# Splitting an attention output projection around the first block of running maxima, and reordering VectorE's work beside it

## The chip, the core and the metric

The kernel runs on one core of one Trainium2 chip. A core has four computing engines with instruction streams of their own: TensorE (PE, matrix products, written to PSUM banks), VectorE (DVE), ScalarE (ACT) and GpSimd (POOL). A fifth stream, SyncE (SP), issues most DMA transfers. The engines meet only at semaphores. The metric is the device time of one execution in microseconds; the median of several runs counts.

## The reference

Sixteen sequences of 512 tokens with 256 features go through one attention layer and one mixture-of-experts layer.

```
x = layernorm(x + attention(x))        # 16 heads of 16; each token sees 39 earlier offsets: 0..32, 48, 64, 96, 128, 192, 256, 384
    scores = q . shift(k, offset) / 4 + pos_bias ; alpha = softmax(scores)
    out    = (sum alpha * shift(v, offset)) * sigmoid(x @ Wgate + bgate) @ Wout + bout
x = layernorm(x + experts(x))          # router: relu(x @ rw1) @ rw2, top 2 of 8, capacity 1024; two-layer experts
```

Products are made from half-precision pairs: a value is split in a high and a low half, and three products (high by high, high by low, low by high) are added up.

## The kernel before

Three stages follow one another: `attention` with the router and the scatter of the tokens (to about 1300 us), `experts`, and `combine`, the last normalization. The change is in `attention` alone.

Attention works on one sequence, a batch, at a time, in a software pipeline written out by hand. An iteration has 16 slots. The table `SLOTS_OF` says which parts stand in a slot, and `AHEAD` of which batch: while the projections (`proj`) and the maxima (`maxp`) are those of the next batch, the scores and values are those of this one, and the gate, the output projection (`outp`) and the router (`rout`, `rank`) those of the last or the one before. Each engine walks through the same slots. TensorE does a part in its own slot, the others one slot later, or by as many as `LATER` says. Within a slot an engine first does what its `head` function finds in the tables, then the parts in their listed order, and then, on ScalarE, its `tail`. A slot is no barrier: it only fixes the order in which each engine issues its work, and the semaphores do the rest. An engine that waits holds up all that is behind it in this order.

These parts stand around the change:

- **Output projection.** Part `t` transposes the gated attention output and ScalarE copies it to `featT` (L860). Part `w` (L754 on TensorE) multiplies by `wout`: 24 products, two PSUM banks of 12. VectorE adds the residual (L1036), takes statistics of the four row tiles (`bn_stats` L1041, `bn_aggr` L1044), GpSimd makes the inverse deviation (L1147 to L1152), and ScalarE normalizes (part `y`, L909) and casts (L914). Then comes the router, from the same rows.
- **Near maxima, `near0` to `near3`, far maxima, `far0` and `far1`.** TensorE computes scores of the next batch (L720 for the bias, L730 the products; L740 and L748 for far), two banks each, and VectorE takes the maximum of each group (L1022, L1026).
- **Six pairs of score and value blocks, k = 0 to 5** (two far, four near), placed by the tables `SCORES_AT` to `EVAC_AT`. For a pair TensorE makes the scores (`scores`), ScalarE the exponentials (`weights`, L831 and L832, `EXP_AT`), VectorE and GpSimd the low halves, one half of the heads each (`split_weights`, L415, `SPLIT_AT`), and TensorE multiplies by the values (`values`, L666, `VALUES_AT`). A far result is copied by ScalarE (`evacuate_far`, L823), a near one is added by VectorE to what came back of the far results (`merge`, L958 and L963); both follow `EVAC_AT`.
- **The way of the far results.** SyncE's head at slot 6 waits for both far copies, stores `o_far` to memory in four transfers (L465), waits until they have landed, and loads them in another order as `o_back` (L468). The first near merge waits for this load. SyncE issues ahead of it the row loads of the next batch's queries and keys (L500).

All projections, maxima and transposes share three PSUM banks `gp` in rotation. Each use takes the bank of the third use before it, once that has been drained by its reader (`unit` on TensorE, `gp_drained`). `near` parts acquire both their banks before their first product:

```
units = [unit(n, "maxp", part, e) for e in range(2)]
```

A near value block can only begin when the merge of the one before it is done, since there is one pair of banks `o`:

```
alone.wait_ge(plo_dve, n.at(UNIT_PAIRS, k + 1))
alone.wait_ge(plo_pool, n.at(UNIT_PAIRS, k + 1))
...
    alone.wait_ge(merged, n.at(TILES, k - FAR_PAIRS))
```

The orders that result in this stretch are, before the change:

- TensorE: output projection, near0, values 2, scores 3, near1, near2, near3, far0, values 3, scores 4, far1, router transposes.
- VectorE: split 2, rank, two residual adds, statistics, near0, first near merge, near1, split 3, near2, near3, `y` low half, far0, rank, second merge, far1.
- ScalarE: gate and value casts, `featT` copies, exponentials 2, copy of far result 1, `y`, exponentials 3.

Of the kernel before, what the change touches and what calls it, by code (L numbers as in the profile page):

```python
# [57 lines left out]
SLOTS_OF = {  # L58
    0: [("proj", "qk0"), ("gate", "den1"), ("gate", "inv1")], 1: [("proj", "qk1"), ("gate", "mul")], 2: [("proj", "vg0")],
# [12 lines left out]
         ("dve", "rout", "h0"): 2, ("dve", "rout", "h1"): 2, ("dve", "rout", "h2"): 2, ("dve", "rout", "h3"): 2}  # L72

UNITS = {("feat", "x"): 2, ("proj", "qk0"): 2, ("proj", "qk1"): 2, ("proj", "vg0"): 2, ("proj", "vg1"): 2,
         ("outp", "t"): 2, ("outp", "w"): 2, ("maxp", "near0"): 2, ("maxp", "near1"): 2, ("maxp", "near2"): 2,
         ("maxp", "near3"): 2, ("maxp", "far0"): 2, ("maxp", "far1"): 2,
         ("maxp", "t"): 1,
         ("rout", "t"): 2, ("rout", "h0"): 2, ("rout", "h1"): 2, ("rout", "h2"): 2, ("rout", "h3"): 2,
         ("rank", "l"): 1, ("rank", "c"): 1}

SCORES_AT = [-1, 0, 5, 7, 10, 12]
EXP_AT = [[-1, 1, 5, 8, 11, 13], [0, 1, 5, 8, 11, 13]]
SPLIT_AT = [1, 2, 6, 9, 12, 14]
VALUES_AT = [2, 4, 7, 10, 13, 16]
EVAC_AT = [3, 5, 8, 11, 14, 16]

GATED = {"den0": (0, 2), "inv0": (0, 2), "den1": (2, 4), "inv1": (2, 4)}
GATE_STEPS = len(GATED)
# [43 lines left out]
def wait(eng, sem, value):  # L132

    if not isinstance(value, int) or value > 0:
        eng.wait_ge(sem, value)
# [122 lines left out]
def attention(nc, g):  # L258
    ctx = ExitStack()
    with ctx:  # L260
# [160 lines left out]
        def _(sync):  # L421
# [18 lines left out]
            def head(n, h):  # L440
                if (n.c, h) == (B, 2):
                    first_expert()
                if not n.in_range():
                    return
                if h == 0 and n.shift(2).in_range() and not (n.i is None and n.c + 2 >= B):
                    load_x(n.shift(2))
                if h == 1:

                    wait(sp, pv_done, n.at(UNIT_PAIRS))
                    sp.wait_ge(v_stored, n.at(16, 16))  # L450
                    if n.i is None and n.c == 0:
                        sp.wait_ge(pad_in, 32)
                    for u in range(2):
                        half = PAIRS * VW
                        src = bass.AP(v_dram[n.par].tensor, half * u, [[2 * half, 2 * BLOCK], [2 * half * BLOCK, N // BLOCK], [1, half]])
                        dst = v_near[2 * BLOCK * u:2 * BLOCK * (u + 1), :, u, :, :]
                        sync.dma_start(dst.rearrange("w b h c -> w b (h c)"), src).then_inc(v_near_in, 16)
                if h == 6:

                    wait(sp, o_in, n.at(16))  # L460
                    sp.wait_ge(far_out, n.at(FAR_PAIRS, FAR_PAIRS))
                    for r4 in range(4):
                        dst = o_dram.rearrange("(a g r) c -> r a g c", g=4, r=4)[r4]
                        src = o_far[BLOCK * r4:BLOCK * (r4 + 1), :, :, :].rearrange("a g h c -> a g (h c)")
                        sync.dma_start(dst, src).then_inc(o_stored, 16)  # L465
                    wait(sp, merged, n.at(TILES))
                    sp.wait_ge(o_stored, n.at(64, 64))
                    sync.dma_start(o_back[:, :, :, :].rearrange("p t h c -> p t (h c)"), o_dram.rearrange("(t p) c -> p t c", p=P)).then_inc(o_in, 16)  # L468
                if h == 9:

                    if n.i is not None or n.c > 0:
                        drained(sp, n.shift(-1), "outp", "w", 1)
                    sync.dma_start(xres[:, :, :], g["x_rows"][bass.ds(n.at(N), N), :].rearrange("(t p) d -> p t d", p=P)).then_inc(xres_loaded, 16)

            def proj(n, part):
# [88 lines left out]
        def _(pe):  # L564
# [189 lines left out]
            def outp(n, part):  # L754
                if part == "t":
                    pe.wait_ge(og_hi, n.at(1, 1))
                    transposes(n, "outp", "t", 0, lambda t, c: og16[:, 0, t, P * c:P * (c + 1)])
                    pe.wait_ge(og_lo, n.at(1, 1))
                    transposes(n, "outp", "t", 1, lambda t, c: og16[:, 1, t, P * c:P * (c + 1)])
                elif part == "w":  # L760
                    drained(pe, n, "outp", "t", 0)
                    drained(pe, n, "outp", "t", 1)
                    for u in range(2):
                        bank, is_full = unit(n, "outp", "w", u)
                        for t in (2 * u, 2 * u + 1):
                            last = terms(lambda a, c: featT[:, a, c, P * t:P * (t + 1)], lambda b, c: wout[:, b, c, :],
                                         bank[:, D * (t % 2):D * (t % 2 + 1)])
                        last.then_inc(is_full, 1)
# [45 lines left out]
        def _(act):  # L814
# [101 lines left out]
            def rout(n, part):  # L916
                if part == "t":

                    transposed(n, "rout", lambda: full(act, n, "outp", "w", 1))
                else:  # L920
                    for k in range(2):
                        ht = 2 * int(part[1]) + k
                        bank = full(act, n, "rout", part, k)
                        wait(act, hid_lo, n.at(HT, ht - 3))
                        if ht == 0:

                            act.wait_ge(qk_split, n.at(4, 12) if n.i is not None else min(n.at(4, 12), 4 * B))
                        if ht == 0 and n.i is None and n.c == 0:
                            act.wait_ge(biases_in, 80)
                        if ht == 0 and (n.i is not None or n.c > 0):  # L930
                            full(act, n.shift(-1), "rank", "l", 0)
                        nc.scalar.activation(hid16[:, 0, ht, :], bank[:, :], ACT.Relu, bias=br1[:, ht:ht + 1], scale=1.0 / WS)  # L932
                        gp_done(nc.scalar.activation(rows32[:, ht % 4, :], bank[:, :], ACT.Relu, bias=br1[:, ht:ht + 1], scale=1.0 / WS),  # L933
                                n, "rout", part, k)
# [10 lines left out]
        def _(dve):  # L945
# [81 lines left out]
                                                        AX.X, ALU.max, negate=True), n, "maxp", part, e)  # L1027

            def outp(n, part):
                if part == "w":  # L1030
                    wait(dve, y_stored, n.at(16))
                    wait(dve, yh_ready, n.at(1))
                    for u in range(2):
                        bank = full(dve, n, "outp", "w", u)
                        dve.wait_ge(xres_ready, n.at(1, 1))
                        gp_done(nc.vector.scalar_tensor_tensor(y32[:, 2 * u:2 * u + 2, :], bank[:, :].rearrange("q (t d) -> q t d", t=2), 1.0 / WS,  # L1036
                                                               xres[:, 2 * u:2 * u + 2, :], ALU.mult, ALU.add), n, "outp", "w", u)
                    for u in range(2):
                        drained(dve, n, "outp", "w", u)
                    for t in range(TILES):  # L1040
                        nc.vector.bn_stats(stats[:, t, :], y32[:, t, :]).then_inc(ln_step, 1)  # L1041
                    alone.wait_ge(ln_step, n.at(TILES, TILES))
                    for t in range(TILES):
                        nc.vector.bn_aggr(mv[:, t, :], stats[:, t, :]).then_inc(var_ready, 1)  # L1044
                elif part == "y":
                    dve.wait_ge(yh_ready, n.at(1, 1))
                    nc.vector.tensor_tensor(y16[n.par][:, :, D:2 * D], y32[:, :, :], y16[n.par][:, :, 0:D], ALU.subtract).then_inc(yl_ready, 1)
# [76 lines left out]
        def _(gpsimd):  # L1124
# [13 lines left out]
            def outp(n, part):  # L1138
                if part == "t":

                    pool.wait_ge(xres_loaded, n.at(16, 16))
                    if n.i is None and n.c == 0:
                        pool.wait_ge(biases_in, 80)
                    nc.gpsimd.tensor_tensor(xres[:, :, :], xres[:, :, :], g_bo, ALU.add).then_inc(xres_ready, 1)
                elif part == "w":
                    pool.wait_ge(var_ready, n.at(TILES, TILES))
                    nc.gpsimd.tensor_scalar(veps[:, :], mv[:, :, 1], LN_EPS, 0.0, ALU.add, ALU.max)  # L1147
                    nc.gpsimd.tensor_scalar(nmr[:, :], mv[:, :, 0], -1.0, 0.0, ALU.mult, ALU.add).then_inc(veps_ready, 1)
                    pool.wait_ge(veps_ready, n.at(1, 1))
                    nc.gpsimd.tensor_tensor(rstd[:, :], veps[:, :], halfneg[:, :], ALU.pow).then_inc(rstd_ready, 1)  # L1150
                    pool.wait_ge(rstd_ready, n.at(1, 1))
                    nc.gpsimd.tensor_tensor(nmr[:, :], nmr[:, :], rstd[:, :], ALU.mult).then_inc(nmr_ready, 1)  # L1152
# [557 lines left out]
```

## Time and profile before

| what | value |
|---|---|
| median of 3 runs | 1766.84 us (1765.27 to 1768.31) |
| the profiled execution | 1772.04 us, of which the span from first to last instruction is 1770.3 us |
| TensorE busy, of the span | 1355.1 us (77%) |
| VectorE, ScalarE, GpSimd busy | 968.0, 902.0, 711.6 us |
| mean granted TensorE clock | 0.793 of full speed |

A row of the timeline gives the start in us from the span's start, the duration, engine, line, operation, output and input, and how many instructions are merged in it. In brackets stands how long the engine sat idle before it, and what ended that idle time. "issue" means that the engine waited for nothing that the profile shows. PE stands for matrix products and PEld for weight loads. A window row gives the stretch, its length, the busy time of each engine with its instructions, the granted clock (1.00 is 2.4 GHz, 0.50 is 1.2 GHz), and the DMA share and rate.

### The profile page before, as it was taken

Reading aid. Unit: us, or ns where it says so; the run is one execution under the profiler, and the core shown is the slowest. Engines: PE = TensorE matmul, PEld = TensorE weight load, DVE = VectorE, ACT = ScalarE, POOL = GpSimd, SP = SyncE. Lnnn points to the kernel's source line nnn. Section 1 sums busy time; section 2 is a strip of 40 time slices with the busy share of each in tenths; the row PEclk is TensorE's granted clock in tenths of the full one; section 3 lists DMA queues with packets and bytes.
Section 4 is the critical chain, followed back from the end, with each engine's and each line's share of the span. In section 5 each row is a group of like instructions: output and inputs, shape, how many; then the busy total and the mean of one; then the engine's idle time right before and its main releaser. Section 6 shows DMA issues by size and latency. Waiting matters only on the chain. (4 is left out here: it accounts for less than half of the span.)

```text
span 1770.3 us, 69102 instructions
## 1 busy us (share of the span) xinstructions
PE 1355.1 (77%) x31232; PEld 867.7 (49%) x31232; DVE 968.0 (55%) x2079; ACT 902.0 (51%) x1551; POOL 711.6 (40%) x653
## 2 busy tenths in 40 slices
PE   3556687786978888787787969787753999999960
PEld 1334354444545454555455545454432666666640
DVE  3225456564656755566565746656553555555426
ACT  4134364453746546464544636454543655555517
POOL 5123144353636445364443626344332133333346
PEclk9567696777868778787777869676766999999985
DMA  7655263533426353453634425252322344444239
GB/s 198 167 143 126 84 150 86 128 95 106 118 76 162 89 126 90 100 126 89 151 71 112 96 83 140 67 137 54 103 37 86 84 96 96 96 96 96 37 36 380
DMA packets 194694, 195.49 MB, mean 110 GB/s; under 512 B 61711, under 2 KB 178527, under 8 KB 191152
## 3 DMA queue, kind: packets, MB, share of 16 engines
q1 hardware_dynamic: 176208, 167.44, 35.9%
q0 software_dynamic: 15360, 15.10, 5.5%
q10 hardware_dynamic: 2832, 8.52, 1.2%
q8 instruction: 246, 4.03, 1.0%
q14 instruction: 48, 0.39, 0.1%
HBM read 115.63 MB, written 86.25 MB: 114 GB/s over the span
## 5 line engine op out<-in xcount | busy, mean ns | idle before, releaser
L415 POOL TENSOR_TENSOR p<-p 128x512 f16<-128x512 f32 x96 | 130.2, 1356 | 262.7 <-ACT p L832 262.6
L860 ACT COPY featT<-gp 128x1024 f16<-128x1024 f16 x96 | 93.0, 1023 | 270.3 <-PE gp L577 270.3
L1169 POOL DMA_INDIRECT disp<-y,sidx x128 | 187.8, 1467 | 55.7 <-issue 37.8
L1441 POOL DMA_INDIRECT xln<-y,place x64 | 103.4, 1615 | 222.3 <-DVE y L1581 203.7
L584 PE MATMUL gp<-featT,wr 128*128 128x512 f16 x768 | 186.0, 398 | 5.2 <-issue 2.9
L415 DVE TENSOR_TENSOR p<-p 128x512 f16<-128x512 f32 x96 | 83.0, 865 | 194.0 <-ACT p L832 193.9
L831 ACT ACTIVATE p<-st 128x512 f16<-128x512 f32 x192 | 116.8, 609 | 79.1 <-PE st L629 45.5
L1538 ACT ACTIVATE h<-up,v_near 128x512 f16<-128x512 f32 x128 | 88.2, 689 | 130.8 <-issue 124.0
L1156 POOL TENSOR_TENSOR x<-xin,x 128x1024 f16<-128x1024 f32 x16 | 34.0, 2127 | 276.1 <-ACT x L867 276.1
L1591 DVE TENSOR_TENSOR h<-h 128x512 f16<-128x512 f32 x128 | 88.7, 694 | 72.8 <-ACT h L1539 72.8
L629 PE MATMUL st<-qs,ks 49*64 49x32 f16 (+1 forms) x4096 | 102.2, 197 | 33.0 <-issue 32.9
L584 PEld LDWEIGHTS gp<-featT,wr 128*128 128x128 f16 x768 | 73.1, 101 | 100.8 <-issue 24.0
L584 PE MATMUL gp<-featT,wqk 128*128 128x512 f16 x384 | 115.9, 473 | 6.6 <-issue 5.5
L832 ACT ACTIVATE p<-st 128x512 f32<-128x512 f32 x192 | 118.0, 615 | 0.0
L932 ACT ACTIVATE hid<-gp,br 128x512 f16<-128x512 f32 x128 | 90.6, 708 | 53.3 <-DVE hid L1054 27.8
L1054 DVE TENSOR_TENSOR hid<-rows,hid 128x512 f16<-128x512 f32 x128 | 103.9, 855 | 14.2 <-ACT rows L933 14.2
L1005 DVE RECIPROCAL og<-og 128x512 f32<-128x512 f32 x32 | 107.3, 3353 | 1.1
L1131 POOL TENSOR_TENSOR qk<-rows,qk 128x512 f16<-128x512 f32 x64 | 73.5, 1157 | 82.3 <-ACT rows L884 81.8
L958 DVE TENSOR_TENSOR ob<-o,o_back 128x136 f32<-128x136 f32 x128 | 31.9, 291 | 133.1 <-DMA o_back<-o_dram 96.6
L1022 DVE TENSOR_REDUCE m_near<-gp 128x8 f16<-128x512 f32 x128 | 81.8, 680 | 30.7 <-PE gp L730 30.5
L629 PEld LDWEIGHTS st<-qs,ks 49*64 49x64 f16 (+1 forms) x4096 | 67.9, 120 | 58.9 <-issue 36.5
L1026 DVE TENSOR_REDUCE m_far<-gp 128x16 f16<-128x512 f32 x64 | 41.2, 686 | 94.4 <-PE gp L748 94.4
(191 smaller groups left out, 3046.1 us busy)
## 6 DMA issues: line engine op xcount, KB each, us to landing
v_near<-v_dram SPq DMA_DIRECT2D x32, 528.0 KB, 7.8
qk_dram<-qk SPq DMA_DIRECT2D x64, 256.0 KB, 3.6
o_dram<-o_far SPq DMA_DIRECT2D x64, 136.0 KB
o_back<-o_dram SPq DMA_DIRECT2D x16, 544.0 KB, 4.2
v_dram<-vs SPq DMA_DIRECT2D x16, 528.0 KB, 3.2
v_far<-v_dram SPq DMA_DIRECT2D x64, 132.0 KB
disp<-y ACTq DMA_DIRECT2D x8, 1040.0 KB, 7.1
rows<-disp SPq DMA_DIRECT2D x16, 520.0 KB, 3.6
```

Of the source, the lines that this page charges most:

```text
L415: engine.tensor_tensor(p16[:, b, 1, :], p32[:, b, :], p16[:, b, 0, :], ALU.subtract).then_inc(is_split, 1)
L584: last = nc.tensor.matmul(dst, lhs(a, c), rhs(b, c), start=(k == 0), stop=(k == len(todo) - 1))
L629: last = nc.tensor.matmul(banks[e][64 * u + first:64 * (u + 1), P * z + BLOCK * b:P * z + BLOCK * (b + 1)], key[rows[e], p, lo - BLOCK + f ...
L831: nc.scalar.activation(p16[:, b, 0, :], bank[:, :], ACT.Exp)
L832: nc.scalar.activation(p32[:, b, :], bank[:, :], ACT.Exp).then_inc(exp_ready, 1)
L860: gp_done(nc.scalar.copy(featT[:, i, :, :].rearrange("f c t -> f (c t)"), bank[:, :].bitcast(F16)), n, stage, PART_OF_T[stage], i)
L932: nc.scalar.activation(hid16[:, 0, ht, :], bank[:, :], ACT.Relu, bias=br1[:, ht:ht + 1], scale=1.0 / WS)
L1005: nc.vector.reciprocal(v, v).then_inc(og_step, 1)
L1054: nc.vector.tensor_tensor(hid16[:, 1, ht, :], rows32[:, ht % 4, :], hid16[:, 0, ht, :], ALU.subtract).then_inc(hid_lo, 1)
L1169: nc.gpsimd.indirect_dma_start(out=disp[:, :], out_offset=bass.IndirectOffsetOnAxis(ap=sidx[:, t, k:k + 1], axis=0), in_=y16[n.par][:, t, ...
L1441: nc.gpsimd.indirect_dma_start(out=xln[:, :], out_offset=bass.IndirectOffsetOnAxis(ap=place[:, gr, t:t + 1], axis=0), in_=y[:, gr, t, :], ...
L1591: nc.vector.tensor_tensor(h16[:, gr, 1, h, :], h32[:, h % 2, :], h16[:, gr, 0, h, :], ALU.subtract).then_inc(h_lo, 1)
```

## The change

The output projection becomes two parts, `w0` and `w1`, one bank each, with near0 between them. The residual add goes with each, and the statistics become a part of their own, `s`, behind both, for VectorE and GpSimd. VectorE's order becomes: residual add 0, near0, residual add 1, statistics, near1, first near merge, near2, near3, split 3, `y` low half, far0. On TensorE scores 3 move behind near1, and values 3 ahead of far0. On ScalarE the copy of far result 1 moves ahead of the second half of the value casts, the `featT` copies and exponentials 2. SyncE's reload of `xres` waits for `w1` in place of the second bank of `w`. The bank rotation changes with the order: near0 now takes banks between those of w0 and w1.

```
-    6: [("outp", "w"), ("maxp", "near0")],
+    6: [("outp", "w0"), ("maxp", "near0"), ("outp", "w1"), ("outp", "s")],
...
-         ("outp", "t"): 2, ("outp", "w"): 2, ("maxp", "near0"): 2, ...
+         ("outp", "t"): 2, ("outp", "w0"): 1, ("outp", "w1"): 1, ("maxp", "near0"): 2, ...
...
-SCORES_AT = [-1, 0, 5, 7, 10, 12]
+SCORES_AT = [-1, 0, 5, 8, 10, 12]
-SPLIT_AT = [1, 2, 6, 9, 12, 14]
-VALUES_AT = [2, 4, 7, 10, 13, 16]
-EVAC_AT = [3, 5, 8, 11, 14, 16]
+SPLIT_AT = [1, 2, 6, 10, 12, 14]
+VALUES_AT = [2, 4, 7, 9, 13, 16]
+EVAC_AT = [3, 4, 9, 11, 14, 16]
...
-                        drained(sp, n.shift(-1), "outp", "w", 1)
+                        drained(sp, n.shift(-1), "outp", "w1", 0)
...
-                elif part == "w":
-                    drained(pe, n, "outp", "t", 0)
-                    drained(pe, n, "outp", "t", 1)
-                    for u in range(2):
-                        bank, is_full = unit(n, "outp", "w", u)
+                elif part[0] == "w":
+                    if part == "w0":
+                        drained(pe, n, "outp", "t", 0)
+                        drained(pe, n, "outp", "t", 1)
+                    for u in (int(part[1]),):
+                        bank, is_full = unit(n, "outp", part, 0)
...
             def outp(n, part):
-                if part == "w":
-                    wait(dve, y_stored, n.at(16))
-                    wait(dve, yh_ready, n.at(1))
-                    for u in range(2):
-                        bank = full(dve, n, "outp", "w", u)
-                        dve.wait_ge(xres_ready, n.at(1, 1))
-                        gp_done(nc.vector.scalar_tensor_tensor(..., n, "outp", "w", u)
-                    for u in range(2):
-                        drained(dve, n, "outp", "w", u)
+                if part[0] == "w":
+                    if part == "w0":
+                        wait(dve, y_stored, n.at(16))
+                        wait(dve, yh_ready, n.at(1))
+                        dve.wait_ge(xres_ready, n.at(1, 1))
+                    u = int(part[1])
+                    bank = full(dve, n, "outp", part, 0)
+                    gp_done(nc.vector.scalar_tensor_tensor(..., n, "outp", part, 0)
+                elif part == "s":
+                    for u in range(2):
+                        drained(dve, n, "outp", f"w{u}", 0)
                     for t in range(TILES):
                         nc.vector.bn_stats(stats[:, t, :], y32[:, t, :]).then_inc(ln_step, 1)
```

On GpSimd the part `w` is renamed to `s`. No instruction is added or taken away on any engine.

## Rows read from the trace of the kernel before

**Rows 1.** Busy time of TensorE on the page: us, share, instructions.

```profile
PE 1355.1 (77%) x31232; PEld 867.7 (49%) x31232; DVE 968.0 (55%) x2079; ACT 902.0 (51%) x1551; POOL 711.6 (40%) x653
```

**Rows 2.** Waits over the span: waiting line, releaser, us, times, longest.

```profile
DVE ob L958 <- DMA o_back<-o_dram: 96.6, 16, 12.8
...
PE gp L720 <- DVE m_near L1022: 77.7, 33, 9.6
...
PE gp L740 <- DVE m_near L1022: 14.2, 16, 0.9
```

**Rows 3.** Timeline of TensorE in batch A, projection at 944.11.

```profile
944.11 2.78 PE L584 MATMUL gp<-wout,featT 128*128 128x256 f16 x24
946.88 0.39 PE L720 MATMUL gp<-near_bias,sel_rest 32*128 32x512 f16 x2
...
948.09 0.73 PE L666 MATMUL o<-v_near,p 128*32 128x66 f16 x64
...
952.41 0.39 PE L720 MATMUL gp<-near_bias,sel 32*128 32x512 f16 x2
...
958.64 0.61 PE L720 MATMUL gp<-near_bias,sel 32*128 32x512 f16 x2 [5.20 <-DVE m_near L1022]
...
962.96 0.39 PE L740 MATMUL gp<-far_bias,sel 32*128 32x256 f16 x2 [0.88 <-DVE m_near L1022]
...
967.06 0.82 PE L666 MATMUL o<-v_near,p 128*32 128x34 f16 x57 [1.67 <-issue]
967.81 0.29 PE L624 MATMUL st<-sel,near_bias 64*128 64x128 f16 x2
```

**Rows 4.** Timeline of VectorE in batch A.

```profile
946.92 0.69 DVE L1036 SCALAR_TENSOR_TENSOR y<-gp,xres 128x512 f32<-128x512 f32 x1 [0.19 <-PE gp L584]
...
949.16 0.38 DVE L1044 BATCH_NORM_AGGREGATE mv<-stats 128x2 f32<-128x6 f32 x4
...
956.86 0.51 DVE L958 TENSOR_TENSOR ob<-o,o_back 128x136 f32<-128x136 f32 x2 [6.15 <-DMA o_back<-o_dram]
```

**Rows 5.** Timeline of ScalarE in batch A.

```profile
940.67 0.42 ACT L892 CAST vs<-vg 128x256 f16<-128x256 f32 x1 [3.54 <-DVE vg L982]
...
941.91 1.90 ACT L860 COPY featT<-gp 128x1024 f16<-128x1024 f16 x2
...
945.84 0.71 ACT L823 COPY o_far<-o 128x272 f32<-128x272 f32 x2
...
951.58 2.07 ACT L909 ACTIVATE y<-y,nmr,rstd 128x256 f32<-128x256 f32 x4 [4.93 <-POOL nmr L1152]
...
956.13 0.61 ACT L832 ACTIVATE p<-st 128x512 f32<-128x512 f32 x1
```

**Rows 6.** Timeline of SyncE's DMA issues in batch A.

```profile
944.30 0.89 SPq L500 DMA_DIRECT2D ks<-qk_dram  x2
946.62 2.54 SPq L465 DMA_DIRECT2D o_dram<-o_far  x4
952.29 0.38 SPq L468 DMA_DIRECT2D o_back<-o_dram  x1
```

**Rows 7.** Timeline of GpSimd in batch A: its half of split 3.

```profile
956.82 1.16 POOL L415 TENSOR_TENSOR p<-p 128x512 f16<-128x512 f32 x1 [5.28 <-ACT p L832]
```

**Rows 8.** Timeline of TensorE in batch B, projection at 717.34.

```profile
717.34 4.45 PE L584 MATMUL gp<-wout,featT 128*128 128x256 f16 x24
...
730.12 0.61 PE L720 MATMUL gp<-near_bias,sel 32*128 32x512 f16 x2 [2.74 <-DVE m_near L1022]
```

**Rows 9.** Timeline of ScalarE in batch B: the last of exponentials 3.

```profile
731.03 0.61 ACT L832 ACTIVATE p<-st 128x512 f32<-128x512 f32 x1
```

**Rows 10.** Timeline of VectorE in batch B: the first near merge.

```profile
728.35 0.50 DVE L958 TENSOR_TENSOR ob<-o,o_back 128x136 f32<-128x136 f32 x2 [2.74 <-DMA o_back<-o_dram]
```

**Rows 11.** Windows in batch A: PE, PEld, DVE, ACT, POOL busy, clock, DMA share, GB/s.

```profile
952.00:954.00 2.00, 1.44 (x96) 0.95 (x84) 0.00 (x0) 1.91 (x5) 0.00 (x0) 0.78 0.26 49
958.00:979.00 21.00, 14.23 (x558) 9.94 (x559) 10.50 (x29) 2.80 (x4) 0.00 (x0) 0.50 0.04 11
```

More of the change, by code:

```diff
@@ L74 @@
 UNITS = {("feat", "x"): 2, ("proj", "qk0"): 2, ("proj", "qk1"): 2, ("proj", "vg0"): 2, ("proj", "vg1"): 2,
-         ("outp", "t"): 2, ("outp", "w"): 2, ("maxp", "near0"): 2, ("maxp", "near1"): 2, ("maxp", "near2"): 2,
+         ("outp", "t"): 2, ("outp", "w0"): 1, ("outp", "w1"): 1, ("maxp", "near0"): 2, ("maxp", "near1"): 2, ("maxp", "near2"): 2,
          ("maxp", "near3"): 2, ("maxp", "far0"): 2, ("maxp", "far1"): 2,
@@ L917, in rout @@
                 if part == "t":
-                    transposed(n, "rout", lambda: full(act, n, "outp", "w", 1))
+                    transposed(n, "rout", lambda: full(act, n, "outp", "w1", 0))
                 else:
@@ L1029, in outp @@
             def outp(n, part):
-                if part == "w":
-                    wait(dve, y_stored, n.at(16))
-                    wait(dve, yh_ready, n.at(1))
-                    for u in range(2):
-                        bank = full(dve, n, "outp", "w", u)
-                        dve.wait_ge(xres_ready, n.at(1, 1))
-                        gp_done(nc.vector.scalar_tensor_tensor(y32[:, 2 * u:2 * u + 2, :], bank[:, :].rearrange("q (t d) -> q t d", t=2), 1.0 / WS,
-                                                               xres[:, 2 * u:2 * u + 2, :], ALU.mult, ALU.add), n, "outp", "w", u)
-                    for u in range(2):
-                        drained(dve, n, "outp", "w", u)
+                if part[0] == "w":
[5 more added lines that the diff above has]
+                    bank = full(dve, n, "outp", part, 0)
+                    gp_done(nc.vector.scalar_tensor_tensor(y32[:, 2 * u:2 * u + 2, :], bank[:, :].rearrange("q (t d) -> q t d", t=2), 1.0 / WS,
+                                                           xres[:, 2 * u:2 * u + 2, :], ALU.mult, ALU.add), n, "outp", part, 0)
+                elif part == "s":
+                    for u in range(2):
+                        drained(dve, n, "outp", f"w{u}", 0)
                     for t in range(TILES):
@@ L1144, in outp @@
                     nc.gpsimd.tensor_tensor(xres[:, :, :], xres[:, :, :], g_bo, ALU.add).then_inc(xres_ready, 1)
-                elif part == "w":
+                elif part == "s":
                     pool.wait_ge(var_ready, n.at(TILES, TILES))
```

## The prediction

> **What bounds the kernel.** I read four views: the page's busy times, the list of waits, the timelines of two batches engine by engine, and windows for the clock. The chain that ended last is no help, since it covers only the last stage, which the change leaves alone. TensorE is busy for 1355.1 us [rows 1], and in every steady iteration of attention it is the engine with the least idle time, so a microsecond of its idle time is worth about one of the total, if the wait is not put back elsewhere. The list of waits shows where its idle time is: before near1 to near3 it stood 77.7 us, and before far0 14.2 us, until VectorE's near maxima had drained a bank [rows 2]. That is 91.9 us over the 15 iterations that make near maxima for a next batch, 6.1 us each. VectorE isn't slow there, it is stuck. Its first near merge stood 96.6 us, 16 times, for the reload of the far results [rows 2], and near1's maxima are queued behind this merge.
>
> Two batches show the range. In batch A TensorE ends near1 at 953.4 and stands 5.20 us before near2, 0.88 before near3 and 0.88 before far0, 6.96 in all [rows 3]. (The 0.88 before near3 is not among the rows; it is the same wait on the near reduction as before far0.) VectorE had waited 6.15 us for the load and merged at 956.86 [rows 4]. In batch B the first of these waits is 2.74 us [rows 8], so 4.50 in all, with the merge at 728.35 [rows 10].
>
> **What is moved, and what is late next.** The change adds no instruction. Its whole effect is which wait ends last. I follow batch A.
>
> *ScalarE's copy of far result 1* costs 0.71 us [rows 5], and it is moved ahead of the second value casts, the `featT` copies and exponentials 2. ScalarE was idle for 3.54 us before 940.67 [rows 5], but values 1 end only about 0.3 us before that, so only some 0.2 us of the copy is covered. I charge about 0.5 us to the `featT` copies, which end at 943.81 and release the projection at 944.11 [rows 3, 5]: TensorE starts it 0.3 us late. Exponentials 2 and split 2 are as late.
>
> *The way of the far results* gets earlier. The copy ended at 946.55 and SyncE stored at 946.62 [rows 5, 6]. Now the copy ends near 941.2, and SyncE is held by its own row loads until 945.19 [rows 6]. So the stores can start 1.4 us earlier and no more. They meet these loads in the DMA engines, so the gain at landing lies between 0 and 1.4 us, and I take 0.7. The load itself took 4.57 us from issue to merge [rows 4, 6]. The store of `y` and the reload of `xres`, which were issued during it, come later now, so I take another 0.4 off, with 0 and 0.7 as ends. The data is there at 955.8 in place of 956.86.
>
> *The projection halves.* 24 products took 2.78 us, near0 1.21 [rows 3]. The sum stays. w0 ends at 945.85, near0 at 947.05, and w1, which needs the bank that residual add 0 drains at about 947.2, ends at 948.65. VectorE does near0's maxima in 1.25 us from 947.2, residual add 1 to 949.45, and the statistics to 951.3, against 949.54 before [rows 4]: 1.8 us later. All of the chain to GpSimd, `y` and exponentials 3 is late by this 1.8. They ended at 956.74 [rows 5] and now end at 958.5. GpSimd's half of split 3 takes 1.16 us [rows 7] and ends at 959.7.
>
> *TensorE.* Values 2 and near1 run without a wait to 950.3, scores 3 with their 1.9 us of "issue" to 953.9, and near2 finds its banks drained: the 5.20 us are gone. near2 ends at 955.0. VectorE did near1's maxima by 952.6 and merges at 955.8 for 1.0 us. It reads near2's first bank by 957.5, and only then can near3 start: a wait of 2.5 us. near3 ends at 958.8, its maxima at 960.1, and VectorE's half of split 3, now queued behind them, at 960.8. Values 3, which stood behind far0 and so had far0 as cover, now start there: a wait of 2.0 us. From here 1.0 us of values and 2.16 us of far0 (962.96 to 965.12) bring scores 4 to 964.1, without any issue stall. Before it was 967.81, less the 1.67 of "issue" [rows 3], 966.1. Batch A gains 2.0 us: 6.96 of waits go, and 0.3, 2.5 and 2.0 come.
>
> *Batch B* was less late at the merge, while its exponentials 3 ended at 731.64 [rows 9]. Its projection ran at half clock, 4.45 us [rows 8]. Here the statistics are 1.3 us later, exponentials 3 end at 732.95, GpSimd's split at 734.1, and 3.2 us behind it scores 4 start at 737.3. Before, far0 started 4.3 us behind near2, as in A, at 734.4, and scores 4 without issue stalls at 737.6. It gains 0.3 us, as the chain through `y` decides it.
>
> *The sum.* The mean wait of 6.1 us per batch lies between B's 4.5 and A's 6.96, at 0.65 of the way, so the mean gain is 0.3 + 0.65 x 1.7 = 1.4 us, in 15 iterations 21 us. While TensorE stands at a semaphore, its instruction stream can catch up. Stalls named "issue" (1.90 in the middle of scores 3, 1.67 in values 3 of batch A) lie in the blocks of tiny products, and now values 2, near1, scores 3 and near2 follow one another without a pause. I charge 0.3 us a batch, 4 us, between 0 and 1 us a batch. No other wait takes over later in the iteration: the far maxima, the router transposes, the transposed maxima and the row loads behind them keep their order and all shift together. The profiled execution would go from 1772.04 to 1755, by 0.96%. On the median 1766.84 this is 1750.
>
> **The clock.** TensorE's granted clock was already at a mean of 0.78 of full speed in 952 to 954, while near1 still ran, and stayed at 0.50, 1.2 GHz, from 958 to 979 [rows 11]. In this stretch the engine was busy for 14.23 us, with tiny products in the main. So the fall began before the 5.20 us stand, and I count on no help from its going. The Trainium skill (TensorE: Matmul & The Clock Gate, Part 1) says that idle time brings the clock down to 1.2 GHz and sustained activity back up. By it, cutting the long stand in two would keep 2.4 GHz, and the sum would be near 1711; by the rows it stays at 1750.
>
> **Rivals.**
>
> 1. *The clock stays up.* The longest stand falls from 5.2 to some 2.5 us. near1 at 2.4 GHz took 1.03 us, near2 at 1.2 GHz 1.28 by the same timeline: a fifth. Of the 14.23 us in the low stretch some 2.8 would go, in 14 batches 39 us, so 1711, and with part of it 1711 to 1733. For it: the stand is the longest idle time of the iteration. Against: the clock at 952 to 954, and that it doesn't rise in the busy part of the 21 us.
>
> 2. *The output projection no longer lifts the clock (slower).* Batch B's projection began at 1.2 GHz and took 4.45 us, and the clock rose within or behind it. Cut in two by near0, it may leave the clock down until the router's hidden layer. Then w1 costs 0.8 more, near0, values 2 and near1 0.7, and scores 3 0.5, about 2 us a batch, and the statistics are later by most of it, which puts values 3 off by another 1. Three times 14 is 42 us against a gain of 17: 1792 at the worst, and 1771 where only the half of the batches that are like B suffer. It decides from 1.2 us a batch on.
>
> 3. *A wait for a wait (no change).* Values 3 without far0 as cover may wait as long as near2 did. In B it nearly does. If the far results land no earlier and exponentials 3 are late by 1 us more than I count, A gains 0.5 us and B loses 0.7: 1764 to 1769.
>
> **How the numbers follow.** Forecast, a gain of 0.3 to 1.9%: 0.62. Rival 1: 0.10. Rival 2: 0.14. Rival 3: 0.14. The bounds of the sum are 0.4 to 2.2 us a batch, 1734 to 1761. The range reaches to rival 3, to 1768, and on the low side to 1733, and leaves rivals 1 and 2 outside for the most part. A change of 0.2% (3.5 us) is about what a measurement of this kernel can tell from none. Faster: the forecast, rival 1 and a little of rival 3, 0.73. Same: most of rival 3 and the edge, 0.12. Slower: 0.15.
>
> **What the profile after would show.** Right: no wait of the near1 and near2 bias products (L720) on the near maxima above 1 us, one before near3 of 1 to 3 us, none before far0; a wait of 2 to 4 us of values 3 (L666) on a split (L415); the first merge's wait for the load down from 6 to about 3 us; ScalarE's `y` 1 to 2 us later after the start of the projection; scores 4 starting near 20 us after the start of the projection in batches like both A and B, where it was 22.0 in A without the issue stall. Wrong: if values 3 wait over 5 us, if the low clock starts with the projection in most batches, or if new "issue" time eats the gain.

## The result, and the profile after

The changed kernel takes 1759.91 us in the median of 20 runs, the kernel before 1767.68 in 20 runs beside them. The ratio is 0.9949, with a 95% interval from 0.9931 to 0.9966: 0.5% faster. Forecast were 1750 us and 0.96%, with a range from 1733 to 1768. The time is inside the range and the sign is right; the gain, 7.8 us by the medians, is about half of what was forecast, and its interval excludes 0.96%. The two executions that were profiled took 1772.04 and 1759.34 us, 12.7 us apart, since the one of the kernel before ran 4 us longer than its median.

The list of waits of the changed kernel. Its lines L720 and L740 are still the near and far bias products, L666 the values, L1023 the near maxima and L959 the first instruction of a merge:

```profile
DVE ob L959 <- DMA o_back<-o_dram: 44.8, 14, 6.9
...
PE gp L720 <- DVE m_near L1023: 31.1, 18, 5.4
...
PE o L666 <- DVE p L415: 28.7, 14, 2.5
...
PE o L666 <- POOL p L415: 14.3, 3, 9.7
```

The stand before the near products fell from 77.7 us in 33 waits to 31.1 in 18, and that before far0 (14.2) is gone but for one of 0.9 [rows 2]. In its place values 3 wait for a split. Of the 14.3 us for GpSimd's half, 9.7 us are one wait in the last iteration, where near maxima no longer exist; the kernel before had 9.0 us there.

Now one batch like A, with the projection at 325.91. TensorE:

```profile
325.91 1.47 PE L584 MATMUL gp<-wout,featT 128*128 128x256 f16 x12
327.96 0.39 PE L720 MATMUL gp<-near_bias,sel_rest 32*128 32x512 f16 x2 [0.59 <-DVE taken L1091]
...
329.10 1.48 PE L584 MATMUL gp<-wout,featT 128*128 128x256 f16 x12
...
334.27 0.70 PE L730 MATMUL gp<-ks,qs 16*32 16x64 f16 x59 [2.61 <-issue]
...
337.89 0.60 PE L720 MATMUL gp<-near_bias,sel 32*128 32x512 f16 x2
...
340.73 0.61 PE L720 MATMUL gp<-near_bias,sel 32*128 32x512 f16 x2 [1.55 <-DVE m_near L1023]
...
343.08 0.25 PE L730 MATMUL gp<-ks,qs 16*32 16x64 f16 x8 [1.14 <-issue]
345.34 0.36 PE L666 MATMUL o<-v_near,p 128*32 128x66 f16 x16 [2.01 <-DVE p L415]
...
348.36 0.29 PE L624 MATMUL st<-sel,near_bias 64*128 64x128 f16 x2
```

near2 (337.89) starts without a wait, near3 waits 1.55 us, values 3 wait 2.01. A wait of 0.59 us before near0 is new: its second bank was drained by the rank part, which stands behind split 2 on VectorE. It came 3 times, 1.8 us in all. Scores 4 (348.36) start 22.5 us after the projection, not near the forecast 20; three issue stalls of this batch, two of which are shown, take 4.3 us. VectorE and ScalarE of the same batch:

```profile
332.86 0.38 DVE L1047 BATCH_NORM_AGGREGATE mv<-stats 128x2 f32<-128x6 f32 x4
...
338.95 0.51 DVE L959 TENSOR_TENSOR ob<-o,o_back 128x136 f32<-128x136 f32 x2 [2.66 <-DMA o_back<-o_dram]
```

```profile
322.08 0.68 ACT L824 COPY o_far<-o 128x272 f32<-128x272 f32 x2 [3.05 <-PE o L657]
...
323.88 1.92 ACT L861 COPY featT<-gp 128x1024 f16<-128x1024 f16 x2
...
335.28 2.07 ACT L910 ACTIVATE y<-y,nmr,rstd 128x256 f32<-128x256 f32 x4 [7.42 <-POOL nmr L1155]
...
339.84 0.61 ACT L833 ACTIVATE p<-st 128x512 f32<-128x512 f32 x1
```

The statistics end 7.3 us after the projection's start in place of 5.4 [rows 4], exponentials 3 at 14.5 in place of 12.6 [rows 5]. The first merge starts at 13.0; in A it was 12.75. SyncE shows why it isn't earlier:

```profile
326.53 0.89 SPq L500 DMA_DIRECT2D ks<-qk_dram  x2
327.51 2.53 SPq L465 DMA_DIRECT2D o_dram<-o_far  x4
334.90 0.38 SPq L468 DMA_DIRECT2D o_back<-o_dram  x1
```

The far stores start 1.6 us after the projection's start in place of 2.5 [rows 6], yet the reload is issued at 9.0, where it was 8.2 in A.

The next table is worked out from the timelines, as means over 12 iterations from the second projection on, in us per iteration. "Work" is the time from the projection's start to scores 4 less all waits and stalls in it. The columns are the kernel before, the changed one, and four of the runs below: VectorE's order alone, the change without the halves and the early copy, VectorE's order with the early copy and the far results first, and the change without the halves with the row loads late. Each column is one execution. In the order of the columns these took 4.4 us more, and 0.6, 0.2 and 6.1 less than the median of their kernel, 8.9 more and 8.6 less. So a column can be off by 0.6 us per iteration from what the kernel does as a rule.

```
                                before  changed  order  no halves  order, far first  late loads, early copy
iteration                        76.8     76.0    75.9     75.0         77.3               74.6
waits before near and far0        5.1      1.4     3.0      2.7          2.6                2.0
wait of values 3                  0.0      2.2     0.0      2.0          0.0                2.0
issue stalls                      8.7      9.0    10.0      7.4         11.1                7.8
projection to scores 4           23.8     23.1    22.9     22.9         24.2               22.1
  work in it                     14.6     15.2    14.9     14.9         15.2               14.7
reload issued after projection    8.3      8.0     7.9      8.4          1.7                1.6
first merge after projection     12.7     12.8    12.7     12.8         14.7               10.1
```

### The profile page after: what moved, and what is told of

Same layout as the page of the kernel before. It is cut to its first block and busy times, and to the rows that moved or that the text cites. A ratio compares the mean times of both kernels' runs of the same rounds, so it can differ in the third digit from the quotient of the medians.

```text
span 1757.6 us, 69086 instructions
## 1 busy us (share of the span) xinstructions
PE 1364.2 (78%) x31232; PEld 867.5 (49%) x31232; DVE 971.1 (55%) x2079; ACT 902.0 (51%) x1551; POOL 712.1 (41%) x653
## 5 line engine op out<-in xcount | busy, mean ns | idle before, releaser
L1023 DVE TENSOR_REDUCE m_near<-gp 128x8 f16<-128x512 f32 x128 | 82.2, 684 | 59.3 <-PE gp L730 58.6
L584 PE MATMUL gp<-featT,wqk 128*128 128x512 f16 x384 | 111.2, 458 | 4.8 <-issue 3.6
L1057 DVE TENSOR_TENSOR hid<-rows,hid 128x512 f16<-128x512 f32 x128 | 102.8, 847 | 12.6 <-ACT rows L934 12.6
L910 ACT ACTIVATE y<-y,nmr,rstd 128x256 f32<-128x256 f32 x64 | 33.2, 588 | 137.2 <-POOL nmr L1155 137.2
L666 PE MATMUL o<-v_near,p 128*32 128x66 f16 (+1 forms) x4096 | 52.8, 204 | 59.6 <-DVE p L415 28.7
L629 PEld LDWEIGHTS st<-qs,ks 49*64 49x64 f16 (+1 forms) x4096 | 68.1, 120 | 51.7 <-issue 29.3
```

The lines of the kernel that those rows point to most:

```text
L584: last = nc.tensor.matmul(dst, lhs(a, c), rhs(b, c), start=(k == 0), stop=(k == len(todo) - 1))
L629: last = nc.tensor.matmul(banks[e][64 * u + first:64 * (u + 1), P * z + BLOCK * b:P * z + BLOCK * (b + 1)], key[rows[e], p, lo - BLOCK + f ...
L1057: nc.vector.tensor_tensor(hid16[:, 1, ht, :], rows32[:, ht % 4, :], hid16[:, 0, ht, :], ALU.subtract).then_inc(hid_lo, 1)
```

## The experiments

All ratios are to the kernel before, of runs on the same chip, with 95% intervals.

### VectorE's order alone (`e1_dve_order`)

The edit on the kernel before:

```
-SPLIT_AT = [1, 2, 6, 9, 12, 14]
-EVAC_AT = [3, 5, 8, 11, 14, 16]
+SPLIT_AT = [1, 2, 6, 10, 12, 14]
+EVAC_AT = [3, 5, 9, 11, 14, 16]
```

> The kernel before with VectorE's order alone changed: the first near merge behind near1's maxima, and split 3 behind near3's. Projection in one piece, values 3 behind far0, far copy where it was. Theory A (the gain is VectorE's order; the projection halves and values 3 ahead of far0 only cost): the statistics stay at 5.4 or 7.1 us after the projection's start, the wait before near2 goes, one of about 2 us before near3 stays, values 3 wait for nothing since far0 covers them, scores 4 gain 2 us or more per batch, ratio 0.980 to 0.988. Rival B (the gain needs the near0 maxima and near1 earlier, which only the halves give): ratio 0.997 to 1.000.

Measured: 0.992 (0.9891 to 0.9948). Rival B falls: two entries of the tables give what the whole change gives, and more by the central value, though the intervals overlap. Theory A has the place right and the size too large. Its list of waits:

```profile
PE gp L720 <- DVE m_near L1022: 38.1, 33, 4.7
...
PE st L629 <- issue: 34.7, 20, 3.3
...
PE gp L730 <- issue: 18.9, 16, 2.9
```

The stand before near fell by 39.6 us [rows 2]. The stalls named "issue" before near products (L730) alone rose from 9.0 to 18.9 us, and all of them from 8.7 to 10.0 us per iteration by the table.

### The halves alone (`e2_halves`)

The edit is the changed kernel with the four tables (`SCORES_AT`, `SPLIT_AT`, `VALUES_AT`, `EVAC_AT`) of the kernel before.

> The projection halves and the statistics behind residual add 1 alone, all tables as before. Theory A: the statistics come 1.9 us later, the stand before near2 stays as long as it was, since the merge still waits for the load ahead of near1's maxima: ratio 1.000 to 1.004. Rival B: the earlier near0 maxima shorten the stands, ratio 0.995 to 0.998.

Measured: 1.0091 (1.0059 to 1.0122), slower by twice what theory A gave it, and rival B falls again. The windows from the projection's start to the end of w1 in two of its batches (us, then busy PE, PEld, DVE, ACT, POOL, the clock, DMA share and GB/s):

```profile
942.39:948.75 6.36, 6.36 (x98) 3.70 (x94) 2.94 (x6) 2.54 (x7) 1.81 (x2) 0.55 0.99 246
405.55:410.20 4.65, 4.05 (x102) 2.88 (x102) 2.94 (x6) 2.54 (x7) 1.81 (x2) 1.00 0.99 247
```

The same work takes 4.65 us at 2.4 GHz, with 0.6 of idle time in it, and 6.36 at a clock of 0.55. That the statistics come 1.9 to 2.1 us later shows in its trace. But this one profiled execution took 1773.8 us, 11 below the median of its runs, so it does not show where the rest of the 0.9% is.

### The changed kernel with one part back (`e3_values_back`, `e4_copy_back`)

```
-VALUES_AT = [2, 4, 7, 9, 13, 16]
+VALUES_AT = [2, 4, 7, 10, 13, 16]
```

> The changed kernel with values 3 again behind far0 on TensorE, all else as changed. Theory A: the wait of 2.0 us of values 3 on the split goes under far0 in nearly every batch, 30 us in all of which issue stalls take back a third: ratio 0.983 to 0.989 to the kernel before. Rival C (TensorE's time is filled by issue stalls and a lower clock whatever wait goes): ratio 0.993 to 0.996, as the changed kernel.

Measured: 0.9942 (0.9912 to 0.9972), as the changed kernel. Rival C holds. The list of waits has no wait of values 3 on VectorE's split in the steady iterations any more, but:

```profile
PE gp L720 <- DVE m_near L1023: 32.8, 19, 7.3
...
PE gp L730 <- issue: 30.3, 19, 2.7
...
PE o L666 <- issue: 29.3, 19, 3.3
...
PE gp L740 <- DVE m_near L1023: 14.2, 16, 0.9
```

Of the 2.2 us per iteration of values 3, 0.8 stands before near and far0 again and 1.2 more is "issue" (10.2 against 9.0). The lower clock that rival C names as well did not come: the work up to scores 4 is 14.6 us here, against 15.2. The values' own issue stalls rose from 16.4 to 29.3 us in all.

```
-EVAC_AT = [3, 4, 9, 11, 14, 16]
+EVAC_AT = [3, 5, 9, 11, 14, 16]
```

> The changed kernel with the copy of far result 1 where it was, behind exponentials 2. The changed kernel's trace has the stores 1.5 us earlier but the reload issued as late as before. Theory A: the early copy gives nothing and costs the 0.3 us start of the projection, so taking it back is worth 0 to 5 us: ratio 0.992 to 0.995. Rival D (the early copy pays, the load would be later still without it): the merge starts 1 us or more later, ratio 0.997 to 1.003.

Measured: 0.9914 (0.9884 to 0.9944). This is below theory A's range. Taking the early copy back is worth 0.35% by the central values, though the intervals overlap, and rival D falls: the reload was issued at 8.2 us in the mean (8.0 with the early copy) and the merge started at 12.5, no later than with it (12.8).

### The way of the far results (`e5_far_first`, `e6_order_far_first`, `e8_small_loads`)

In the first two kernels the row loads leave the end of `proj` and come behind the far reload. The first is otherwise the changed kernel, the second the kernel with VectorE's order alone and the early copy.

```
+            def load_rest(n):
+                sp.wait_ge(qk_lo_stored, n.at(32, 32))
+                ...            (the four row loads, as they stood in proj)
...
+                if h == 7 and n.shift(1).in_range():
+                    load_rest(n.shift(1))
```

> The changed kernel, and on SyncE the store and the reload of the far results are issued ahead of the four row loads of the next batch's queries and keys instead of behind them. Theory A (these loads hold back the landing of the stores, so that the early copy of far result 1 comes to nothing): the reload is issued 2 to 3 us after the projection's start in place of 8.4, the merge follows near1's maxima at about 9 to 10 in place of 13, the wait before near3 falls to 0.9 us, values 3 still wait 2 us for the split; ratio to the kernel before 0.985 to 0.992. Rival E (the stores are slow for themselves, whatever is issued ahead): reload at 6 us or later and ratio 0.993 to 0.997.

Measured: 0.994 (0.9917 to 0.9963). The mechanism of theory A is right and its price wrong. SyncE in a batch with the projection at 240.33:

```profile
237.26 3.44 SPq L474 DMA_DIRECT2D o_dram<-o_far  x4
242.65 0.37 SPq L477 DMA_DIRECT2D o_back<-o_dram  x1
243.06 0.96 SPq L445 DMA_DIRECT2D qs<-qk_dram  x2
```

The reload is issued at 2.3 us, 1.7 in the mean. The merge starts at 10.2 in the mean in place of 12.8, the wait before near3 falls from 1.4 to 0.9 us, and issue stalls rise from 9.0 to 9.7.

> VectorE's order alone, as in the run of that name, with the early copy of far result 1 and the far store and reload ahead of the row loads; the projection in one piece, values 3 behind far0. Theory A: no stand before near2 and only 0.9 us before near3 and far0 each, nothing before values 3; of the 2 us of waits that go, half comes back as issue stalls; ratio 0.975 to 0.986. Rival E: ratio 0.990 to 0.994, as VectorE's order alone.

Measured: 0.9985 (0.9964 to 1.0006). Theory A falls for this kernel, and rival E's number does not hold either. TensorE and SyncE where the row loads now are:

```profile
260.39 0.40 PE L633 MATMUL st<-qs,ks 49*64 49x32 f16 x15 [5.54 <-issue]
```

```profile
250.37 0.36 SPq L477 DMA_DIRECT2D o_back<-o_dram  x1
250.78 0.97 SPq L445 DMA_DIRECT2D qs<-qk_dram  x2
251.79 0.89 SPq L445 DMA_DIRECT2D ks<-qk_dram  x2
```

Five transfers are issued from 250.4 to 252.7, and TensorE stands from 254.85 to 260.39 in the middle of scores 3 with nothing to wait for that the profile shows. With near1 behind it, the merge is late at 14.7 though its data has long been there. Five of the 12 iterations have such a stall, of 4.4 to 5.5 us, each behind or beside the same five transfers. In the kernel before no issue stall of the first 12 us was above 3.3 us, and they came to 2.2 us per iteration; here they are 3.1.

In the third the row loads stay where they were in the changed kernel, and shrink:

```
+                full_rows = n.c < 2
...
+                        top = MROW if full_rows else HD + 1
+                        sync.dma_start(dst[n.par][STACK * e + HD:STACK * e + top, :, :]..., src[0:top - HD, :]).then_inc(rest_in[n.par], 16)
```

> The changed kernel with the four row loads of queries and keys cut to one row each from the third batch on (the low halves of scores are then those of an early batch). It takes about 480 KB of traffic out of each iteration at the time of the far stores. Theory A: the reload is issued 4 to 5 us after the projection's start in place of 8.4. For the issue stalls: if they come from the instruction stream waiting behind this traffic, they fall from 9.2 to 7 us per iteration or less, and the ratio is 0.97 to 0.98; if they come from the density of the tiny products alone, they stay at 9 us and the ratio is 0.985 to 0.992.

The traffic taken out is about 990 KB per iteration, not 480: the changed kernel's four loads are of 256 KB each, and of 8 KB each here.

Measured: 0.9888 (0.9857 to 0.9919). The reload is issued at 5.0 us in the mean in place of 8.0, after stores issued 0.9 us earlier. So most of the 3 us is landing time that the row loads had cost the far stores. Issue stalls stay at 8.9 us. That goes against the idea that this traffic sets them as a rule; the second of the two branches holds.

### Without the halves (`e7_no_halves`, `e9_tables_only`)

The kernel before with the four tables of the change, `EVAC_AT` once as `[3, 5, 9, ...]` and once as `[3, 4, 9, ...]`.

> The changed tables (scores 3 behind near1, values 3 ahead of far0, merge and split later on VectorE) with the projection in one piece and the copy of far result 1 where it was. It differs from the run with the copy back by the halves alone. Theory A: the halves cost (they alone gave 1.009): the statistics are back at 5.4 to 7.1 us, values 3 wait 0 to 1 us; ratio 0.982 to 0.989. Rival F (the cost of the halves depends on the old order, beside the new one they are free or help): ratio 0.991 to 0.996.

Measured: 0.9903 (0.9872 to 0.9933), between the two ranges, beside 0.9914 with the halves. Theory A falls by its wait: the statistics are back at 5.4 to 7.1 us, but values 3 still wait 2.0 us, for VectorE's split behind near3's maxima. So it is VectorE's order, and not the halves, that makes this wait. Rival F is the nearer one: in the new order the halves are free within what can be told.

> The changed kernel's four tables, the early copy of far result 1 among them, with the projection in one piece. Beside the run without the halves (0.990) it differs by the early copy alone, beside the changed kernel by the halves alone. Theory G (the early copy puts the far stores into the row loads, the reload is issued no earlier, and the issue stalls of TensorE between 6 and 18 us after the projection's start grow by 0.5 to 1 us): ratio 0.992 to 0.996, as the changed kernel. Rival F (the halves are what costs in the changed kernel): ratio 0.988 to 0.991.

Measured: 0.9928 (0.9899 to 0.9957), in theory G's range, though the interval reaches into rival F's. The early copy costs 0.25% by the central values; beside the halves it was 0.35%. In both pairs the intervals overlap. Theory G's stalls came at the low end of what it said: 2.6 us between 6 and 18 us, against 2.1 without the early copy. Stores at 0.5 in place of 2.5 us bring the reload to 7.7 in place of 8.4.

### The row loads late (`e10_loads_late`, `e11_late_early`, `e12_before_late`)

The loads move as above, to a later slot and behind a wait for the router's transposes. The first kernel is otherwise the one without halves and early copy, the second has the early copy too, the third is the kernel before.

```
+                if h == 11 and n.shift(1).in_range():
+                    if n.shift(-1).in_range():
+                        full(sp, n.shift(-1), "rout", "t", 1)
+                    load_rest(n.shift(1))
```

> As the run without the halves, with the four row loads of queries and keys issued only when the router's transposes are done, some 30 us after the projection's start, far from the far stores and from the tiny products. Theory H (TensorE's issue stalls come from its instruction stream waiting behind this traffic): the stalls in the first 18 us fall from 2.2 to under 1.5 us an iteration, the reload is issued at 7 us or before; ratio 0.978 to 0.987. Rival I (the density of the tiny products alone sets them): stalls unchanged, ratio 0.987 to 0.992.

Measured: 0.985 (0.9809 to 0.989). The ratio is in theory H's range, but its mechanism is not there: the stalls of the first 18 us are 2.26 us, against 2.14, and the reload is at 7.9. By the timelines TensorE's work between projection and scores 4 is 14.4 us in place of 14.9. 5 of the 12 projections ran at 1.2 GHz for a part in place of 8. Whether that is the loads' doing or this execution's, isn't settled.

> As the run with the row loads late, and the copy of far result 1 early. Theory G: with the row loads out of the way the stores start at -3 us and the reload is issued at 2 to 3 us, the merge follows near1's maxima; ratio 0.974 to 0.986, no worse than without the early copy. Rival (the early copy costs by itself, through the copies that it delays on ScalarE): 0.003 above the run without it.

Measured: 0.9846 (0.9808 to 0.9884), 1739.17 us, the best of all. SyncE in a batch with the projection at 987.61, with no row load near it:

```profile
984.53 3.32 SPq L476 DMA_DIRECT2D o_dram<-o_far  x4
989.81 0.37 SPq L479 DMA_DIRECT2D o_back<-o_dram  x1
```

The reload is issued at 2.2 us, 1.6 in the mean, and the merge starts at 10.1 in the mean, behind near1's maxima. With the loads out of the way, the early copy costs nothing that can be told (0.985 without it), but it pays nothing either; with intervals of 0.004 to each side a cost of 0.003 would not show.

> The kernel before with the row loads alone issued late, as in the other run. Theory H: the far reload comes about 1 to 2 us earlier, the stand before near2 shortens by as much, and the issue stalls of the first 18 us fall by 0.7 us or more: ratio 0.975 to 0.988. Rival I: the stand shortens but the issue stalls take it back: ratio 0.992 to 0.998.

Measured: 0.9966 (0.9939 to 0.9993). The merge starts 0.6 us earlier, the stand before near stays at 5.1 us, issue stalls at 8.7. Rival I gives the right ratio, though neither the stand nor the stalls moved as it said.

## Why the forecast came out as it did

**The bound and the wait** were read rightly. TensorE's stand on the near maxima was VectorE's merge waiting for the far reload: reordering VectorE alone takes 2.2 us per iteration off it and gives the whole gain. The new waits came where they were put: before the near parts 1.4 us in all, before values 3 2.2 (2.0 in nearly every batch). The halves' delay of the statistics, 1.8 us, was 1.9 to 2.1.

**The term that failed first: the far results 1.1 us earlier.** I took 0.7 us from the earlier stores and 0.4 from a freer reload. The changed kernel issues its stores 1.7 us earlier in the mean, the reload 0.3, and merges 0.1 us later. The lower bound, 0, was the truth. The run with small row loads shows what holds the stores: the traffic issued just ahead of them. With 0 in this place, batch A gains 0.9 us in the prediction's own sum, the mean 0.7, and all 15 iterations, less 4 us of stalls, some 6 us (an estimate). Measured were 7.8, so this term alone is as large as the miss.

**The weight of batch A was too large as well.** The mean wait of 6.1 us per batch took in 26 us that stood ahead of the second projection, where the pipeline fills. In the 12 iterations of the table the mean is 5.2, much nearer to B's 4.5 than to A's 6.96.

**Another: TensorE's work held constant.** I kept the sum of projection, near0, values and scores. It rose by 0.6 us per iteration between the projection and scores 4. In 9 of 12 iterations the clock was low for a part of the projection, against 7 of 12 before. One such batch, the stretch from w0 to w1 first, then in parts, with the clock as the third number from the end:

```profile
937.65:944.10 6.45, 6.45 (x100) 3.79 (x104) 2.94 (x6) 1.96 (x5) 2.00 (x2) 0.55 0.95 250
...
926.00:933.00 7.00, 7.00 (x112) 3.98 (x115) 4.57 (x20) 4.78 (x11) 7.00 (x6) 1.00 0.51 112
933.00:938.00 5.00, 4.97 (x210) 4.16 (x195) 1.61 (x4) 4.17 (x10) 3.40 (x4) 1.00 0.55 136
938.50:944.00 5.50, 5.50 (x87) 2.98 (x84) 2.94 (x6) 1.11 (x4) 1.16 (x1) 0.50 0.99 256
```

The projection began at 2.4 GHz here, and the clock fell 0.6 us into it. That is rival 2 in a mild form: such a batch is low for the rest of w0, near0 and w1, and its statistics end at 9.1 us in place of 7.1. The prediction misread batch B in the same way. Its projection did not begin at 1.2 GHz: the clock was 1.00 for the first 0.3 us and then 0.50 for 3.4, to 3.7 us.

How often the clock falls there does not hang on the halves: in 5 to 9 of 12 batches, with them and without. How long it stays low does. In none of the eight kernels with the projection in one piece is it low there for longer than 3.4 us. In the changed kernel it is for 6.8 us or more in 5 of the 12 batches, with the halves alone in 6, in the other four kernels with halves in 1 to 5. But most of the 0.6 us is there without the halves too: the kernel with the tables alone has 15.1 us of work. And in the new order kernels with and without the halves cannot be told apart (0.9914 and 0.9903, 0.9949 and 0.9928). Only in the old order do they cost, 0.9%.

**Issue stalls, 0.3 us a batch,** were 0.3. Per iteration the waits before near and far0 fell by 3.8 us, and smaller waits by 0.3; 2.2 (values 3), 0.3 (issue) and 0.8 (work in the whole iteration) came. This leaves 0.8, the difference of the two profiled executions, 76.8 to 76.0. Forecast were 1.1, and the medians differ by 0.5 (7.8 us in 15 iterations), so where the last 0.3 went one pair of profiles does not tell.

**The cover of values 3** was a true wait with a wrong price. I charged 2.0 us for moving values 3 from behind far0. Moving them back takes this wait away and gives nothing, since issue stalls and the wait before far0 fill the place. And it is no price of the halves' late `y`, as the prediction had it in batches like B: without the halves it is 2.0 us too.

**Rival 1** did not come: the clock was 0.77 in the window where near1 ran, and 0.50 from 336 on.

```profile
332.00:336.00 4.00, 1.73 (x95) 1.37 (x95) 2.19 (x9) 0.72 (x2) 1.70 (x4) 0.77 0.23 68
336.00:354.00 18.00, 11.52 (x550) 7.90 (x543) 9.33 (x30) 4.36 (x8) 1.15 (x1) 0.50 0.31 93
```

The longest wait of this batch for another engine was 2.0 us, against 5.2 in A, and the engine was busy for 11.52 of the 18 us. So cutting the long stand did not keep 2.4 GHz. The Trainium skill (TensorE: Matmul & The Clock Gate, Part 1) names idle time as the cause of the fall. Here an issue stall of 2.6 us lay ahead of it, so this row doesn't speak against the rule, but shortening the semaphore wait was not enough. The batch at 937.65 does speak against idle time as the only cause: TensorE was busy for 11.97 of the 12 us from 926 to 938, and the clock fell 0.3 us later.

**What an issue stall waits for** stands in the kept traces, in the DMA packets of queue 8, which the page calls "instruction" (packets, MB, share of the 16 engines' span):

```profile
q8 instruction: 246, 4.03, 1.0%
```

Each packet has 16 KB. The program has 62464 matrix products and weight loads, 254 for each of the 246 packets. In the kernel before all 66 issue stalls of 0.5 us and more in the 12 iterations end 1.0 to 1.7 us behind the end of such a packet; a moment taken at random does so in 12% of cases. Over all fourteen traces it is 905 of 924. So in these stalls TensorE, by all that the timing shows, waits for its next instructions. In the kernel with the stall of 5.54 us none of these packets moved from 247.39 to 257.75, while the reload and the row loads did; they had been issued from 250.4 on and landed between 255.5 and 259.6. The row loads' volume alone does not set the stalls (small loads left them at 8.9 us). What stays open is when a packet is asked for, and so how far ahead of the tiny products it could come.

## What to carry to other kernels

When an engine stands because a reader is stuck on a slow load, reorder the reader first: two table entries gave the whole gain here, and the split of the projection gave nothing. Issuing a transfer earlier is worth only what lands earlier, so look at what is queued ahead of it; and when a wait goes from a stretch of tiny matrix products, part of it can come back as stalls that no semaphore explains. Then compare them with the packets of the instruction queue.

## What the runs showed of the hardware

- TensorE's long issue stalls end behind an instruction packet of 16 KB: 66 of 66 in the kernel before, 905 of 924 in all. They can fill the place of a wait: where one of 2.2 us per iteration fell, they rose by 1.3 (VectorE's order alone) and 1.2 (values 3 back). Not always: without halves and early copy they fell from 8.7 to 7.4.
- Stores of 4 x 136 KB behind row loads needed 7.2 us from the first issue to the reload's in the changed kernel (0.8 to 8.0) and 5.9 in the kernel before, which issues them 1.7 us later (2.4 to 8.3). With the loads cut to a row or out of the way it was 5.2 us (-0.1 to 5.0, -3.7 to 1.6).
- TensorE's granted clock stood at 0.50 from 336 to 354 while the engine was busy for 11.52 of the 18 us, and it fell at 938.3, though TensorE had been busy for 11.97 of the 12 us up to 938.
